# One-hot rows of a graph kernel: one broadcast comparison a group, the weights moved to the place rows

## What is computed

```python
deg = maximum(segment_sum(ones, dst), 1); d = deg ** -0.5
h = relu(layernorm(x)); feat = h
for i in range(10):                       # hops
    agg = segment_sum(feat[src] * (d[dst] * d[src])[:, None], dst)
    feat = (0.9 * agg + 0.1 * h) * reg[i] + (1 - reg[i]) * feat
x = x + feat
e = relu(layernorm(x))
for _ in range(4):                        # steps
    m = (e @ W_msg.T + b_msg).reshape(n, 4, 128)
    e = gru_cell(segment_sum(m[src, edge_type], dst), e)
return x + e
```

## Time and profile before

| | us |
|---|---|
| median of 3 runs | 2555.01 |
| lowest and highest | 2551.72, 2556.26 |
| the profiled execution | 2550.86 |
| its span, first to last instruction | 2549.3 |
| busy in the span: TensorE, its weight loads | 2190.8, 1440.7 |
| VectorE, ScalarE, GpSimd | 1488.7, 335.0, 134.9 |
| mean granted clock of TensorE | 0.921 of 2.4 GHz |

### The profile page before, as it was taken

How to read it: one execution, slowest core, us unless ns; L and a number is a source line. 1 busy time by engine, 2 the same in 40 slices (tenths; PEclk the granted TensorE clock), 3 DMA queues, 4 the chain that set the end, 5 groups by cost and what they waited for, 6 DMA issues and landing times.

```text
span 2549.3 us, 41289 instructions
## 1 busy us (share of the span) xinstructions
PE 2190.8 (86%) x14375; PEld 1440.7 (57%) x14886; DVE 1488.7 (58%) x3473; ACT 335.0 (13%) x494; POOL 134.9 (5%) x391
## 2 busy tenths in 40 slices
PE   1544545559999999999799999999999999999996
PEld 1322333348999898988644455444554446544464
DVE  6988999977777777777662234522444324442243
ACT  0322223330000000000121011210112100220000
POOL 1322222200000000000000000000000000000000
PEclk9996555559999999999899999999999999999998
DMA  2000000010000000001400000000000000000001
GB/s 72 21 21 21 21 21 21 28 41 2 1 2 2 2 2 2 1 2 49 139 1 1 1 1 1 1 1 1 1 1 1 1 1 1 1 1 1 1 1 50
DMA packets 22188, 34.32 MB, mean 13 GB/s; under 512 B 2450, under 2 KB 18442, under 8 KB 21469
## 3 DMA queue, kind: packets, MB, share of 16 engines
q1 hardware_dynamic: 19025, 30.56, 3.5%
q10 hardware_dynamic: 2944, 0.93, 0.2%
HBM read 18.04 MB, written 13.45 MB: 12 GB/s over the span
## 4 chain that ended last, share of the span: by engine, by line
PE 75%; DVE 15%; issue 5%; DVEq 2%; DMA 2%; ACT 0%; POOLq 0%; ACTq 0%; POOL 0%
PE ps L787 41%; PE ps L706 26%; DVE hot_pair L967 8%; PE ps L739 3%; PE ps L727 2%; DVEq L961 2%; DVE dig L990 1%; DVE hot_place L964 1%; DVE big L993 1%; DMA big<-in_L_gnn_w_hh 1%; PE ps L647 1%; DMA x_after_hops<-x 1%; PE ps L691 1%; PE ps L605 1%; DVE dig L992 1%
## 5 line engine op out<-in xcount | busy, mean ns | idle before, releaser
L787 PE MATMUL ps<-slots,m_parts 125*128 125x500 fp8e4 (+1 forms) x5600 | 1088.0, 354 | 6.6 <-DVE m_parts L1337 5.2
L787 PEld LDWEIGHTS ps<-slots,m_parts 125*128 125x128 f16 x5600 | 547.4, 98 | 495.7 <-issue 10.0
L706 PE MATMUL ps<-parts,big 125*128 125x256 f16 x6125 | 669.6, 273 | 6.8 <-issue 4.2
L706 PEld LDWEIGHTS ps<-parts,big 125*128 125x128 fp8e4 x6125 | 591.3, 98 | 63.6
L605 PE MATMUL ps<-hot_pair,hot_place 125*128 125x228 f16 x1000 | 230.6, 400 | 256.5 <-DVE hot_pair L967 256.5
L1255 DVE TENSOR_SCALAR slots<-big 128x3200 int32<-128x3200 int32 (+1 forms) x112 | 244.1, 2183 | 279.8 <-PE ps L787 279.7
L605 PEld LDWEIGHTS ps<-hot_pair,hot_place 125*128 125x128 f16 x1000 | 143.1, 149 | 343.8 <-DVE hot_pair L967 283.1
L967 DVE TENSOR_SCALAR hot_pair<-iota_pair,win 125x228 f16<-125x228 f16 x1000 | 262.5, 334 | 3.1 <-issue 3.1
L1357 DVE SCALAR_TENSOR_TENSOR r_parts<-ps,over,r_parts 128x500 f16<-128x500 f32 (+1 forms) x28 | 19.1, 684 | 230.1 <-ACT r_parts L527 230.1
L1364 DVE SCALAR_TENSOR_TENSOR gate_r<-ps,over,gate_r 128x500 f32<-128x500 f32 (+1 forms) x28 | 19.1, 682 | 229.3 <-PE ps L739 221.8
L1183 DVE SCALAR_TENSOR_TENSOR hop_tmp<-ps,coef,g 125x128 f32<-125x128 f32 x250 | 87.6, 350 | 97.9 <-PE ps L706 94.4
(11 more groups left out here) (200 smaller groups left out, 1130.2 us busy)
## 6 DMA issues: line engine op xcount, KB each, us to landing
packed_counts<-packed SPq DMA_DIRECT2D x16, 625.0 KB, 3.3
big<-packed_counts SPq DMA_DIRECT2D x4, 1600.0 KB, 7.3
big<-packed_counts SPq DMA_DIRECT2D x3, 1200.0 KB, 6.5
hd<-in_x SPq DMA_DIRECT2D x1, 1562.5 KB
x_again<-in_x SPq DMA_DIRECT2D x1, 1562.5 KB
x_after_hops<-x SPq DMA_DIRECT2D x1, 1562.5 KB
big<-x_after_hops SPq DMA_DIRECT2D x1, 1562.5 KB
out<-big SPq DMA_DIRECT2D x4, 250.0 KB
```

The lines of the kernel that those rows point to most:

```text
L706: last = pe.matmul(ps[:, n % RING, 0:2 * F], tot_f8[0:Q, c, a, :], both((parts0, parts1)[par], a), start=a == 0, stop=a == TILES - 1)
L787: last = pe.matmul(ps[:, k % 2, 0:SIZES[k] * Q], m_parts[0:Q, a, h, t * F:(t + 1) * F], slots_f8[0:Q, t % 2, 0:SIZES[k], a, 0:Q], start=a ...
```

## The change

- The eight pair rows of a group are made by one comparison of 16-bit values, `hot_pair[k, w] = (iota_pair[k, w] == key[w])`, laid out 228 x 8, without weights. For this `iota_pair` becomes 228 x 8, KQ becomes 456, and the staged key is f16.
- The weights go to the place rows. VectorE compares six places (`marks`, 128 x 6) and two (`marks_d`, 128 x 2). ScalarE weighs the six: six activations of 128 elements, read with a step of 6, written contiguously (`weighed`). VectorE weighs the two (`weighed_d`). TensorE reads the moving operand with a step of 8 elements.
- Four buffers (DEPTH) in place of two, for the staged windows, too.
- The digit sum takes five operations: two masks, a sum, a multiplication by 1 + 1/16 on 16-bit values, a last mask.
- ScalarE's order: weigh group j, evacuate group j - 2; the lanes of the block before are split one each behind groups 3, 4 and 5. VectorE runs eight groups ahead of its loop and sums the digits of a block within the next block's groups, behind group 6.
- The general path gets a step that restores the old key spacing.

```diff
-KQ = 1024
+KQ = 456
+KG = 1024
+NOWHERE = -4096.0
+DEPTH = 4
+WA = 6
+WD = W - WA
...
+            win_key = sb("win_key", [128, DEPTH, W], F16, b)
+            win_pw = sb("win_pw", [128, DEPTH, 2, W], F16, b)
+            win_w = sb("win_w", [128, DEPTH, W], F32, b)
-            hot_pair = sb("hot_pair", [128, 2, W, KP], F16, b)
-            iota_pair = sb("iota_pair", [128, KP], F16, b)
+            iota_pair = sb("iota_pair", [128, KP, W], F16, b)
...
+            hot_pair = sb("hot_pair", [128, DEPTH, KP, W], F16, b)
+            marks = sb("marks", [128, DEPTH, 128, WA], F16, b)
+            weighed = sb("weighed", [128, DEPTH, WA, 128], F16, b)
+            marks_d = sb("marks_d", [128, DEPTH, 128, WD], F16, b)
+            weighed_d = sb("weighed_d", [128, DEPTH, 128, WD], F16, b)
...
+            def stage_window(q, b):
+                lo = pool.value_load(windows[0:1, ds(q, 1)], min_val=0, max_val=NCH)
+                pool.wait_ge(s_hot_used, q + 1)
+                pool.tensor_copy(win_pw[0:CH, b, :, :], tab[0:CH, :, ds(lo, W)])
+                pool.tensor_copy(win_w[0:CH, b, :], tab[0:CH, 1, ds(lo, W)])
+                pool.tensor_tensor(win_key[0:CH, b, :], keys[0:CH, ds(lo, W)], q_off[0:CH, ds(q, 1)].broadcast_to([CH, W]),
+                                   ALU.subtract).then_inc(s_wst, 1)
+            with pool.Fori(0, Q // DEPTH) as i:
+                for j in range(DEPTH):
+                    stage_window(DEPTH * i + j, j)
...
             def evacuate(blk, b, j):
                 q = BQ * blk + j
-                act.wait_ge(s_hot_used, W * q + 3 * W)
+                act.wait_ge(s_hot_used, q + 1 + DEPTH)
                 summed(q, extras, s_more_used)
+                if j == 0:
+                    act.wait_ge(s_bytes, blk + 1)
                 act.activation(words[:, b, :, j], ps[:, j, 0:KP], ACT.Copy, scale=float(ONE)).then_inc(s_taken, 1)
...
+            def weigh(q, b):
+                act.wait_ge(s_marks, q + 1)
+                for w in range(WA):
+                    act.activation(weighed[0:CH, b, w, :], marks[0:CH, b, :, w], ACT.Copy,
+                                   scale=win_w[0:CH, b, w:w + 1]).then_inc(s_weighed, 1)
+
+            def block_of(turn, b, n, turn_before):
+                blk = 2 * turn + b
                 for j in range(n):
-                    evacuate(blk, b, j)
-                part_lanes(blk, turn, b, BQ * blk + n - 1)
+                    weigh(BQ * blk + j, j % DEPTH)
+                    if j >= 2:
+                        evacuate(blk, b, j - 2)
+                    elif turn_before is not None:
+                        evacuate(2 * turn_before + 1 - b, 1 - b, BQ - 2 + j)
+                    if 3 <= j < 3 + LANES and turn_before is not None:
+                        part_lane(turn_before, 1 - b, j - 3, 16 * turn_before + BQ * (1 - b) + BQ - 1)
+            block_of(0, 0, BQ, None)
             with act.Fori(0, NB // 2 - 1) as i:
-                block_of(i, 0, BQ)
-                block_of(i, 1, BQ)
...
+                block_of(i, 1, BQ, i)
+                block_of(i + 1, 0, BQ, i)
+            block_of(NB // 2 - 1, 1, Q - (NB - 1) * BQ, NB // 2 - 1)
+            evacuate(NB - 1, 1, 3)
+            part_lane(NB // 2 - 1, 0, 2, BQ * (NB - 1) - 1)
+            evacuate(NB - 1, 1, 4)
+            for l in range(LANES):
+                part_lane(NB // 2 - 1, 1, l, Q - 1)
...
                 pe.wait_ge(s_taken, q + 1)
+                pe.wait_ge(s_pairs, q + 1)
                 for w in range(W):
-                    pe.wait_ge(s_hot, W * q + w + 2 * W + 1)
-                    pe.matmul(ps[:, j, 0:KP], hot_place[0:CH, b, :, w], hot_pair[0:CH, b, w, :],
-                              start=w == 0, stop=w == W - 1, skip_group_check=True).then_inc(s_hot_used, 1)
+                    if w < WA:
+                        pe.wait_ge(s_weighed, WA * q + w + 1)
+                    elif w == WA:
+                        pe.wait_ge(s_weighed_d, q + 1)
+                    place = weighed[0:CH, b, w, :] if w < WA else weighed_d[0:CH, b, :, w - WA]
+                    last = pe.matmul(ps[:, j, 0:KP], place, hot_pair[0:CH, b, :, w],
+                                     start=w == 0, stop=w == W - 1, skip_group_check=True)
+                last.then_inc(s_hot_used, 1)
...
                 dve.wait_ge(s_wst, q + 1)
-                dve.wait_ge(s_hot_used, W * q + W)
-                TT(hot_place[0:CH, b, :, :], iota_place[0:CH, :, :],
-                   win_p[0:CH, b:b + 1, :].broadcast_to([CH, 128, W]), ALU.is_equal)
-                for w in range(W):
-                    TS(hot_pair[0:CH, b, w, :], iota_pair[0:CH, :], win[0:CH, b, 0, w:w + 1],
-                       win[0:CH, b, 1, w:w + 1], ALU.is_equal, ALU.mult).then_inc(s_hot, 1)
+                dve.wait_ge(s_hot_used, q + 1)
+                TT(marks[0:CH, b, :, :], iota_place[0:CH, :, 0:WA],
+                   win_pw[0:CH, b, 0:1, 0:WA].broadcast_to([CH, 128, WA]), ALU.is_equal).then_inc(s_marks, 1)
+                TT(marks_d[0:CH, b, :, :], iota_place[0:CH, :, WA:W],
+                   win_pw[0:CH, b, 0:1, WA:W].broadcast_to([CH, 128, WD]), ALU.is_equal).then_inc(s_marks_d, 1)
+                TT(hot_pair[0:CH, b, :, :], iota_pair[0:CH, :, :],
+                   win_key[0:CH, b:b + 1, :].broadcast_to([CH, KP, W]), ALU.is_equal).then_inc(s_pairs, 1)
+                dve.wait_ge(s_marks_d, q + 1)
+                TT(weighed_d[0:CH, b, :, :], marks_d[0:CH, b, :, :],
+                   win_pw[0:CH, b, 1:2, WA:W].broadcast_to([CH, 128, WD]), ALU.mult).then_inc(s_weighed_d, 1)
...
                 TS(low, x, TWOS, None, ALU.bitwise_and)
                 step(TS(high, x, 2, TWOS, ALU.logical_shift_right, ALU.bitwise_and))
-                step(TT(u16[0], u16[0], u16[1], ALU.add))
-                TS(high, low, NIBBLES, None, ALU.bitwise_and)
-                step(TS(lower, low, 4, NIBBLES, ALU.logical_shift_right, ALU.bitwise_and))
-                step(TT(big1[:, :].bitcast(DT.uint16).rearrange("p (n q) -> p n q", q=64)[:, :, ds(4 * blk, 4)],
-                        u16[1].rearrange("p (n q) -> p n q", q=4), u16[2].rearrange("p (n q) -> p n q", q=4), ALU.add))
+                step(TT(low16, low16, high16, ALU.add))
+                step(TS(high16, low16, 1.0 + 1.0 / 16, None, ALU.mult))
+                step(TS(big1[:, :].bitcast(I32).rearrange("p (n q) -> p n q", q=32)[:, :, ds(2 * blk, 2)],
+                        high.rearrange("p (n q) -> p n q", q=2), NIBBLES, None, ALU.bitwise_and))
                 dve.sem_inc(s_digits, 1)
...
-            HEAD = BQ // 2
-            for j in range(HEAD):
-                onehots(j, j % 2)
+            for j in range(BQ):
+                onehots(j, j % DEPTH)
             with dve.Fori(0, NB // 2 - 1) as i:
                 steps.loop(i, 8)
                 for b in range(2):
                     for j in range(BQ):
-                        onehots(2 * BQ * i + BQ * b + HEAD + j, j % 2)
-                    sum_digits(2 * i + b, b)
+                        onehots(2 * BQ * i + BQ * (b + 1) + j, j % DEPTH)
+                        if j == BQ - 2:
+                            sum_digits(2 * i + b, b)
             steps.done(NB // 2 - 1)
-            for j in range(BQ):
-                onehots(BQ * (NB - 2) + HEAD + j, j % 2)
+            for q in range(BQ * (NB - 1), Q):
+                onehots(q, q % DEPTH)
             sum_digits(NB - 2, 0)
-            for q in range(BQ * (NB - 1) + HEAD, Q):
-                onehots(q, q % 2)
```

More of the change, by code:

```diff
@@ L345, in _ @@
                       allow_small_or_imprecise_dtypes=True).then_inc(s_const, 1)
-            pool.iota(iota_pair[:, :], [[1, KP]], base=0, channel_multiplier=0,
+            pool.iota(iota_pair[:, :, :], [[1, KP], [0, W]], base=0, channel_multiplier=0,
                       allow_small_or_imprecise_dtypes=True).then_inc(s_const, 1)
@@ L366, in stage @@
                 pool.tensor_copy(win_p[0:CH, b, :], tab[0:CH, 0, ds(lo, W)]).then_inc(staged, 1)
[L368 to L371, removed]
+            def stage_window(q, b):
[8 more added lines that the diff above has]
+                    stage_window(DEPTH * i + j, j)
+            for q in range(Q // DEPTH * DEPTH, Q):
+                stage_window(q, q % DEPTH)
             def share_largest():
@@ L385, in _ @@
                           allow_small_or_imprecise_dtypes=True).then_inc(s_iota_g, 1)
+                pool.iota(q_off[:, :], [[KG, QB]], base=0, channel_multiplier=0,
+                          allow_small_or_imprecise_dtypes=True).then_inc(s_iota_g, 1)
+                pool.wait_ge(s_iota_g, 2)
                 with pool.Fori(0, LOADS) as load:
@@ L474, in block_of, with part_lane @@
-            def block_of(turn, b, n):
+            def part_lane(turn, b, l, last):
+                blk = 2 * turn + b
+                if l == 0:
+                    act.wait_ge(s_taken, last + 1 + BANKS)
+                    act.wait_ge(s_digits, blk + 1)
```

(19 more changed lines are left out.)

27 lines of the change are left out of this document (8 added, 19 removed).

## The result

The kernel after takes 2562.56 us (median of nine runs, 2560.17 to 2566.89), the kernel before beside it 2552.99 us (nine runs, 2551.60 to 2556.26). The ratio is 1.0037, 95% interval 1.0027 to 1.0047: about 9.6 us slower, where 25 us less was forecast. The profiled execution took 2566.89 us, the highest of the nine, for 2550.86 before; the two profiled executions lie 16.0 us apart.

A forecast was written before the change was run, and what follows sets the result against it. VectorE bounds the count stage before, ScalarE after; ScalarE's groups, lanes and stops sum to 432.7 us, degree sums start at 509.6 for 534.25, so 25 us off the 2555.0 median gives 2530 us, range 2511 to 2572.

The forecast's parts named there:

- What bounds the kernel before, and VectorE's rows: Count stage: VectorE sets the pace, not TensorE's clock; its group falls to 1.94 us from 2.61, chain to 5.4 from 6.25.
- The new wait: Mid-block, ScalarE idles 4.9 us while VectorE's digit chain delays group 7's marks; 2.5 us more at a turn's end.
- The weighings: ScalarE's six per group, every sixth f16: 0.296 us apart, nothing added for the step; 2.19 us a group with evacuation.
- rival 1: ScalarE's strided weighings slow down: gain gone at 37 ns each; at 51 ns 9 us slower, 2564; chance 0.17.
- costed at nothing: TensorE's eight strided products, at most 2.2 us a group against ScalarE's 3.4, were given no cost in the sum.
- Their covers are the 4.9 us stops: Count stage: ScalarE's stops hide the uncosted work; without them TensorE's 2.3 us a group is near ScalarE's 2.19.
- rival 4: VectorE's comparison loses two elements a cycle, 2649 us; or TensorE's strided products reach 2 ns a column, 2622; chance 0.03 each.
- Number 2: Digit sum's last mask goes at two words a cycle, 0.65 us less in 16 chains, 10 us: 2520; chance 0.15.
- Number 3: ScalarE's register read a group is not hidden: 35 us slower, 2590; chance 0.04.
- The warning on steps: Skill's rule of two hits per 16-byte line for full rate, cited as speaking against the strided weighings and products.

The follow-up runs named there:

- Run 7: Kernel before with only the new, shorter digit sum of five operations: 2541.80 us, ratio 0.9947.
- Run 3: Kernel after with each digit sum moved four groups later in VectorE's order: 2505.63 us, ratio 0.9795 to the kernel before.
- run 1: Kernel after with marks laid out in pairs, so ScalarE reads 4 bytes apart, not 12: 2547.05 us, ratio 0.9960 to the kernel before.
- run 2: Kernel after with hot_pair laid out in pairs, so TensorE's moving operand is read 4 bytes apart, not 16: 2556.93 us, ratio 1.0004 to the kernel before.
- run 4: Kernel after with both marks and hot_pair laid out in pairs: 2515.95 us, ratio 0.9840 to the kernel before.
- run 6: Kernel after with both layouts in pairs, digit sums four groups later, last mask cut into 624 runs and one: 2452.31 us, ratio 0.9598 to the kernel before.

## Why the prediction was wrong, point by point

- **What bounds the kernel before, and VectorE's rows.** Right. The group is 1.97 us (1.94 forecast), the last mask 1.46 (1.45), the multiplication 0.81 (0.80). Run 7 has 5.48 us for a chain where VectorE is the bound (5.4 forecast). One reading beside it was not what it seemed: the turns "at a granted clock of 1.00" and "at 0.53" were compared to show that TensorE's clock does not matter. The first lies ahead of the trace's first clock record (209 us), and TensorE is busy 29.62 and 29.36 us for 128 products in the two, so both ran nearly all at the lower level. That VectorE set the pace is shown by the waits.
- **The new wait.** Right in place and size: 4.51 and 4.87 us (4.9), 2.33 at a turn's end (2.5), released 7.09 and 7.48 us after the chain's start for 7.1; the 0.38 us more in every second block is a gap of 0.53 us before the last mask. Run 3 shows what the wait was worth with TensorE's bound behind it: 57 us.
- **The weighings: the term that failed.** The working took 0.296 us, "I take 0: reading is nearest to the lanes". The lanes read bytes 4 apart, and at 4 bytes this operation indeed costs no more than contiguous (0.290 us apart in run 1, 0.292 in the row). At the kernel's 12 bytes it costs 0.353, 0.061 more. The row of the weights, read 16 bytes apart for 51 ns more, was the nearer one in step; it stood in rival 1 and not in the sum. (The other 13 ns of 0.370 - 0.296 are no cost: one number averages runs of six, the other a run of 25.) A group is 2.46 us and not 2.19; 14 groups a turn are 3.8 of the 4.6 us that the turn was missed by (61.1 for 56.5), and the gap in one chain of two is 0.4. The remaining 0.4 is not assigned.
- **TensorE "costed at nothing": failed as well.** The working allowed 2.2 us for eight strided products and set it against 3.4. They take 3.22, so at the start, where no stop covers them, groups come every 3.22 us and not every 2.19; the first chain starts 9.6 us late. TensorE's share of that is 5.1 us, by run 2; with TensorE fast, the weighings then give another 5.8 (103.88 to 98.04, run 4). "Their covers are the 4.9 us stops" was right only behind the first chain. The evacuation's 2 ns a column, which rival 4 borrowed, was nearer: 0.403 us are 1.77 ns a column.
- **The sum of the misses.** First chain 9.6 us, then 14 blocks with 7 x 0.27 us, 26.5, and 7 gaps of 0.38, 2.7: together 38.8 of the 40.1 us at the degree sums.
- **The rivals.** Number 1 was the main mechanism that happened (the step costs 61 ns, more than the 37 from which it decides); I had given it 0.17. That the 2562.6 us lie so near its 2564 is partly luck. At the measured 57 ns over the forecast's 296 its own sum gives 666 x 0.057 = 38 us, 13 slower, 2568; it has neither TensorE's late start nor the gap in the chain, nor the 0.05 us a group that the evacuation gave back (0.36 for 0.41). The second half of rival 4, the strided products, happened in part. Number 2, the fast mask, did not happen, and run 6 shows why: 625 is odd. The Trainium skill ("VectorE: DVE Perf Modes", What auto-detection actually checks) has "both even or equal" as enough. With 625 on both sides as written the mask took 1456 ns, with 624 it took 825, so the trace disagrees with the rule if the counts reach the engine as written. They may not: the source is contiguous, and if it is handed over as one run of 1250 the counts are neither both even nor equal. No run here separates the two. Number 3 did not happen: ahead of its evacuations ScalarE lost 4.8 us to "issue" in the whole stage.
- **The warning on steps.** The weighings (12 bytes) and the products (16 bytes) both lost rate; at 4 bytes neither did (0.290 us for 0.292 contiguous, 0.190 us for 228 columns). The Trainium skill ("Advanced Engine Details and Errata", SBUF Cachelines) asks for at least two hits on a 16-byte line. Elements 12 or 16 bytes apart give fewer on average, elements 4 bytes apart four, so the runs agree with it on both engines. I cited it and gave it no weight in the sum.

Not settled: the first hop starts 2.6 to 5.2 us later behind the degree sums than in the kernel before in every other trace, run 7 with the old order included, and the part behind the degree sums varies from 2009.5 to 2017.9 us; neither was followed up. What TensorE's 16-byte step costs at the upper clock level was not measured. Whether another split of the eight places between ScalarE and VectorE would gain more was not tried.

## What to carry to other kernels

When an edit widens the step with which an engine reads, price the read from the row with the same step, whatever engine it is, before the row with the same engine and a smaller step; a layout in pairs kept the comparison fast and the reads at 4 bytes. When two bounds lie close together (here 29.3 and 25.8 us a block), removing one shows little (15.5 and 5.6 us here, together 46.6), so test them together as well as apart. A wait for another engine's finished work that stands in the middle of a hand-written order is cheap to move: four groups later gave 57 us.

## What the runs showed of the hardware that was not expected

- ScalarE, 128 f16 elements a partition: operations start 0.353 us apart when read 12 bytes apart, 0.290 when read 4 bytes apart (run 1), 0.292 contiguous.
- TensorE, 228 columns of f16: 0.403 us a product when the moving operand is read 16 bytes apart (clock not recorded there, most likely the lower level); read 4 bytes apart, 0.190 at 0.50 (run 2) and 0.115 at a recorded 1.00 (run 4).
- The clock that the profile prints is 1.00 ahead of the trace's first clock record, whatever the level: run 2 has 33.37 us for 128 products there and 33.34 at 0.50.
- VectorE, 256 elements with two sources: 371 ns when one source comes in runs of two elements 16 bytes apart, 283 ns when contiguous (run 1).
- VectorE, runs of two words written with a stride: 625 runs 1456 ns, 624 runs 825 ns.
